# Graph network with routed experts on one core: places of windows packed four to a word, three row buffers, alternating loads, and the leading window added by VectorE from PSUM

## The reference

```python
# first network: two layers of
summed = segment_sum(x[src], dst); cnt = segment_sum(1, dst)
out = (summed / max(cnt, 1)) @ W_l + b_l + x @ W_r        # relu between the two
x = layernorm(x + out)
# second network: h = x @ W_in + b_in, then for 3 layers
agg = segment_sum(h[src], dst) / max(deg, 1)
logits = concat([h, agg]) @ router_W[l] + router_b[l]     # 8 experts, best two, softmax gates
weak   = relu(agg @ weak_W[l, e] + weak_b[l, e])          # 4 experts
strong = relu(agg @ strong_W1 + b1) @ strong_W2 + b2      # 4 experts, 256 -> 512 -> 256
h = h + sigmoid(h @ conf_W + conf_b) * (gates of the two chosen experts times their outputs, summed)
x = layernorm(x + h @ W_out + b_out)
```

## Time and profile before

| | |
|---|---|
| median of 3 runs | 2573.72 us (2569.99 to 2582.82) |
| the profiled execution | 2555.54 us |
| its span, first to last instruction | 2553.7 us |
| TensorE busy | 2043.9 us (80%) |
| VectorE busy | 907.4 us (36%) |
| ScalarE busy | 578.7 us |
| GpSimd busy | 667.3 us |
| mean granted TensorE clock | 0.859 |

### The profile page before, as it was taken

The page is one execution under the profiler, slowest core; times in us unless marked ns, Lnnn a source line. Parts: engine busy times, 40 slices in busy tenths (PEclk is TensorE's granted clock), DMA queues, the critical chain, the costliest instruction groups (busy, mean ns, idle before and its releaser), DMA issues.

```text
span 2553.7 us, 36575 instructions
## 1 busy us (share of the span) xinstructions
PE 2043.9 (80%) x12522; PEld 1588.1 (62%) x12523; DVE 907.4 (36%) x2327; ACT 578.7 (23%) x1160; POOL 667.3 (26%) x611
## 2 busy tenths in 40 slices
PE   2656666509999899888878999888878999888875
PEld 1345555406767677776656777776756777776664
DVE  5566666442234322533332101333332101333323
ACT  0045555540001000222221000232221100222221
POOL 4133443300000013443330111343330112343330
PEclk9855555559999899999998999899998999899996
DMA  6920000197466755343345432243335432243333
GB/s 175 347 77 0 0 0 0 39 390 263 141 184 226 231 190 190 81 74 59 59 79 212 149 121 75 60 80 59 59 73 210 157 120 77 58 75 63 61 51 103
DMA packets 187286, 298.04 MB, mean 117 GB/s; under 512 B 47952, under 2 KB 153094, under 8 KB 187043
## 3 DMA queue, kind: packets, MB, share of 16 engines
q1 hardware_dynamic: 148786, 237.95, 27.8%
q0 software_dynamic: 38384, 58.53, 12.9%
HBM read 179.30 MB, written 117.13 MB: 116 GB/s over the span
## 4 chain that ended last, share of the span: by engine, by line
PE 63%; DMA 15%; DVE 13%; issue 5%; ACT 2%; SPq 1%; DVEq 0%; POOL 0%; ACTq 0%; POOLq 0%
PE psum L1382 20%; PE psum L1498 13%; DMA arena<-xs_d 12%; PE psum L1296 7%; PE psum L1279 6%; DVE arena L729 4%; PE psum L1461 3%; PE psum L1476 2%; DVE arena L1056 2%; DVE arena L1054 2%; PE psum L1250 2%; DMA adj_d<-arena 1%; PE psum L1301 1%; PE psum L1487 1%; PE psum L1275 1%
## 5 line engine op out<-in xcount | busy, mean ns | idle before, releaser
L1382 PE MATMUL psum<-arena 128*128 128x320 bf16 x3750 | 533.1, 306 | 36.4 <-DMA arena<-adj_d 24.4
L1382 PEld LDWEIGHTS psum<-arena 128*128 128x128 bf16 x3750 | 373.9, 100 | 190.7 <-issue 25.2
L646 POOL DMA_INDIRECT h_rows<-arena,idx x192 | 304.0, 1583 | 558.5 <-DVE arena L1056 515.0
L1487 PE MATMUL psum<-arena 128*128 128x256 f32 x1536 | 361.1, 389 | 3.4 <-ACT arena L1208 3.3
L1498 PE MATMUL psum<-arena 128*128 x1536 | 350.3, 381 | 2.6 <-ACT arena L1211 2.2
L1487 PEld LDWEIGHTS psum<-arena 128*128 128x128 f32 x1536 | 281.3, 193 | 67.9 <-ACT arena L1211 19.0
L1498 PEld LDWEIGHTS psum<-arena 128*128 128x128 f32 x1536 | 285.6, 191 | 40.4 <-issue 5.1
L1211 ACT ACTIVATE arena<-psum,b1c 128x256 f32<-128x256 f32 x384 | 181.8, 474 | 490.5 <-PE psum L1487 490.3
L618 POOL DMA_INDIRECT xs_d<-arena,pos x150 | 145.1, 967 | 549.3 <-DVEq L876 507.3
L1296 PE MATMUL psum<-arena 128*128 128x320 bf16 x1500 | 224.9, 302 | 73.7 <-DMA arena<-adj_d 73.7
L729 DVE TENSOR_TENSOR arena<-arena 125x1600 bf16<-125x1600 bf16 x200 | 229.4, 1190 | 135.3 <-PE psum L1279 133.9
(11 more groups left out here) (250 smaller groups left out, 1681.0 us busy)
## 6 DMA issues: line engine op xcount, KB each, us to landing
arena<-adj_d SPq DMA_DIRECT2D x125, 800.0 KB, 4.5
xs_d<-zrow SPq DMA_DIRECT2D x8, 3432.0 KB, 26.7
arena<-xs_d SPq DMA_DIRECT2D x96, 264.0 KB, 3.4
adj_d<-arena SPq DMA_DIRECT2D x25, 800.0 KB, 7.4
arena<-h_rows SPq DMA_DIRECT2D x22, 640.0 KB, 8.7
h_rows<-zrow SPq DMA_DIRECT2D x1, 8192.0 KB, 38.3
arena<-x_d SPq DMA_DIRECT2D x20, 320.0 KB, 3.6
arena<-in_L_gnn_strong_W SPq DMA_DIRECT2D x24, 256.0 KB, 6.7
```

The lines of the kernel that those rows point to most:

```text
L646: pool.indirect_dma_start(h_rows, bass.IndirectOffsetOnAxis(ap=idx[:, j % 2, h:h + 1], axis=0), ybuf[:, j % 2, h], None, compute_op=ALU.ad ...
L1382: mm = pe.matmul(psum[:, q, 0:HN], hs[:, k * SK + s, part, f * P:(f + 1) * P], half(ring[:, k, s], h), start=(k == 0 and s == 0 and part = ...
L1487: mm = pe.matmul(psum[:, 5 + f % 2, 0:M], w1s[:, j % 2, f // 2, kt, f % 2 * P:(f % 2 + 1) * P], xsT[:, j % 2, kt], start=(kt == 0), stop=( ...
```

## The change

Four edits. The diff below is cut to their core; the removed `adds` is GpSimd's, the new one VectorE's.

1. The places of four windows are packed into one word of four bits each, so `w_rel` has 400 words and not 1600. TensorE loads 16 words once for 8 supersteps and takes each place out with shift, mask and multiplication by WP = 103. The windows now lie 103 columns apart in the two banks.
2. The staging copy on ScalarE and the adds on GpSimd go. VectorE adds the leading window straight from PSUM to `adj`. In each iteration the adds of batch q-1 stand behind the one-hots of batch q, and those of the last batch at the iteration's end. TensorE waits for the add of superstep u-4 too.
3. `xsl` has three buffers. The load of slot j waits for the scaling of slot j-3.
4. Units 3 to 7 of the new states and the five pieces of the next layer's first block are issued in turn.

```diff
-        w_rel = carve([T], I32, 1)
+        w_rel = carve([T // 4], I32, 1)
-        xsl = carve([2, 2, XW], F32)
+        xsl = carve([3, 2, XW], F32)
...
-                    if j > 1:
-                        sp.wait_ge(b_yr, 2 * (J - 1))
-                    sp.dma_start(xsl[:, j % 2], ...
+                    if j > 2:
+                        sp.wait_ge(b_yr, 2 * (J - 2))
+                    sp.dma_start(xsl[:, J % 3], ...
...
-                    if u == 3 and p < 4:
-                        expert_pieces(p + 1, 0)
+                    if u >= 3 and p < 4:
+                        expert_pieces(p + 1, 0, (u - 3,))
...
-            def adds(i):
...
-                    pool.wait_ge(s_stage, i * RS + u + 1)
-                    pool.wait_ge(s_wide, i * RS + u + 1)
-                    pool.wait_ge(s_first, i * RS + u + 1)
-                    a = adj[:, bass.ds(off[u], WC)]
-                    pool.tensor_tensor(a, first_w[:, u % 8], a, ALU.add).then_inc(s_first, 1)
...
                     one_hots(i, q)
+                    if q == 0:
+                        _, off = nc.values_load_multi_w_load_instructions(w_off[0:1, bass.ds(i * RS, RS)], ...
+                    else:
+                        adds(i, q - 1, off)
+                adds(i, NOH - 1, off)
+
+            def adds(i, q, off):
+                for g in range(k):
+                    u = q * k + g
+                    v.wait_ge(s_wide, i * RS + u + 2)
+                    v.wait_ge(s_first, i * RS + u + 1)
+                    a = adj[:, bass.ds(off[u], WC)]
+                    v.tensor_tensor(a, psum[:, u % 4 * 2, 0:WC], a, ALU.add).then_inc(s_first, 1)
...
-                    act.copy(first_w[:, u % 8], banks[:, 0, 0:WC]).then_inc(s_stage, 1)
...
-                    if q % 2 == 0:
-                        n = 2 * k * G
-                        _, rel = nc.values_load_multi_w_load_instructions(
-                            w_rel[0:1, bass.ds(i * (NOH // 2 * n) + q // 2 * n, n)], ...
+                    if q == 0:
+                        _, words = nc.values_load_multi_w_load_instructions(
+                            w_rel[0:1, bass.ds(i * (2 * RS), 2 * RS)], ...
...
                             pe.wait_ge(s_wide, i * RS + u - 2)
+                            pe.wait_ge(s_first, i * RS + u - 2)
...
+                            word = words[2 * u + z // 4]
+                            place = word >> 12 if z % 4 == 3 else (word >> 4 * (z % 4)) & 15 if z % 4 else word & 15
+                            place = nc.s_assert_within(place * WP, 0, G * WP, ...
-                            mm = pe.matmul(bank[:, bass.ds(rel[(q % 2 * k + g) * G + z], WC)], ...
+                            mm = pe.matmul(bank[:, bass.ds(place, WC)], ...
```

More of the change, by code:

```diff
@@ L296, in build @@
         b_tab = sem("slot_tables_ready")
-        b_xin = [sem(f"slot_rows_in_{k}") for k in range(2)]
+        b_xin = [sem(f"slot_rows_in_{k}") for k in range(3)]
         b_turn = sem("slot_turned"); b_xT = sem("slot_turned_taken"); b_w1 = sem("slot_weights_ready")
@@ L459, in _, with expert_pieces @@
                     states(p, b)
-            def expert_pieces(p, b):
+            def expert_pieces(p, b, ks=range(NK)):
                 i = blk(p, b)
-                for k in range(NK):
+                for k in ks:
                     if i == 0:
@@ L715, in _ @@
             link(v.tensor_tensor(w4, w4, base.unsqueeze(2).broadcast_to((1, T // G, G)), ALU.subtract))
-            link(v.tensor_scalar(step_no[0:1, 0:T], wf[:, :], 5.0, float(PAD), ALU.is_ge, ALU.mult))
-            v.scalar_tensor_tensor(w_rel[:, :], wf[:, :], float(WC), step_no[0:1, 0:T], ALU.mult, ALU.add).then_inc(s_tab, 1)
+            four = wf[:, :].rearrange("o (s g) -> o s g", g=4)
+            packed = step_no[0:1, 0:T // 4]
+            link(v.scalar_tensor_tensor(packed, four[:, :, 3], 16.0, four[:, :, 2], ALU.mult, ALU.add))
+            link(v.scalar_tensor_tensor(packed, packed, 16.0, four[:, :, 1], ALU.mult, ALU.add))
+            v.scalar_tensor_tensor(w_rel[:, :], packed, 16.0, four[:, :, 0], ALU.mult, ALU.add).then_inc(s_tab, 1)
             v.wait_ge(s_zero, 2)
@@ L1135, in supersteps @@
                 for u in range(RS):
-                    banks = psum[:, u % 4 * 2:u % 4 * 2 + 2]
+                    banks = psum[:, u % 4 * 2:u % 4 * 2 + 2].rearrange("p b n -> p (b n)")
                     act.wait_ge(s_step, i * RS + u + 1)
-                    if not head or u >= 8:
-                        act.wait_ge(s_first, i * RS + u - 6)
-                    act.copy(first_w[:, u % 8], banks[:, 0, 0:WC]).then_inc(s_stage, 1)
                     act.wait_ge(s_wide, i * RS + u + 1)
-                    act.copy(adj[:, bass.ds(off[u] + WC, G * WC)].rearrange("p (b n) -> p b n", b=2), banks[:, :, WC:WC + GA]).then_inc(s_wide, 1)
+                    act.copy(adj[:, bass.ds(off[u] + WC, G * WC)].rearrange("p (w n) -> p w n", w=G),
+                             banks[:, WP:WP + G * WP].rearrange("p (w n) -> p w n", w=G)[:, :, 0:WC]).then_inc(s_wide, 1)
             supersteps(0, head=True)
@@ L1261, in supersteps @@
                 for q in range(NOH):
-                    if q % 2 == 0:
-                        n = 2 * k * G
-                        _, rel = nc.values_load_multi_w_load_instructions(
-                            w_rel[0:1, bass.ds(i * (NOH // 2 * n) + q // 2 * n, n)], engines=(EPE,), min_val=0, max_val=G * WC + PAD,
-                            skip_runtime_bounds_check_because="a window's offset in its superstep")
+                    if q == 0:
+                        _, words = nc.values_load_multi_w_load_instructions(
+                            w_rel[0:1, bass.ds(i * (2 * RS), 2 * RS)], engines=(EPE,), min_val=0, max_val=0x8888,
+                            skip_runtime_bounds_check_because="four windows' places in a superstep, four bits each")
                     pe.wait_ge(s_oh1, i * NOH + q + 1)
@@ L1278, in supersteps @@
                             n = (g * G + z) // 2
[L1279 removed]
+                            word = words[2 * u + z // 4]
+                            place = word >> 12 if z % 4 == 3 else (word >> 4 * (z % 4)) & 15 if z % 4 else word & 15
+                            place = nc.s_assert_within(place * WP, 0, G * WP, skip_runtime_bounds_check_because="a window's place in its superstep")
+                            mm = pe.matmul(bank[:, bass.ds(place, WC)], oh1[:, q, n, :, z % 2], oh2[:, q, n, :, z % 2],
                                            start=False, stop=(z == G - 1), skip_group_check=True)
```

30 lines of the change are left out of this document (12 added, 18 removed).

## The result

The changed kernel takes 2680.4 us (median of 4 runs, 2677.8 to 2695.2), the kernel before, beside it, 2571.9 us (4 runs, 2564.0 to 2582.8). The ratio is **1.043, 95% interval 1.038 to 1.049**: +109 us. The forecast was 2674 us, inside a range of 2600 to 2725; 86 in 100 stood on slower. The profiled execution took 2677.8 us (span 2676.0), 122 us more than that of before. Its build takes 207 us more from first one-hot to last add (107.3 to 692.5 against 121.8 to 499.7), its slots take 78 us less, and each start of a layer lacks the second wait.

The account below looks back on a forecast made before the run. TensorE's sequencer was taken to bound the build. Build +195, row buffer -82 and queue -12 gave +101 us: the profiled 2555.5 became 2656.5, and with 18.2 to the median 2675, stated as 2674 us, range 2600 to 2725.

Parts of the forecast that it names:

- TensorE's sequencer bounds the build: Build of the adjacency: TensorE's sequencer, not the array or another engine, sets the pace in all 25 iterations, 14.73 us each.
- 0.09 us per ALU operation: Build, TensorE's sequencer: each ALU operation costs 0.09 us, and the change adds 80 to an iteration, 7.2 us.
- 8 semaphore waits, 0.9 us: Build, TensorE: the eight added semaphore waits of an iteration cost 0.11 us each, 0.9 us together.
- Longer fused operations, 0.6 us: Build, TensorE: 64 fused operations an iteration get one or two more steps, 0.01 us each, 0.6 us together.
- Iteration without the end gap, 17.9 us: Build: 8.96 us of supersteps plus 7.2, 0.9, 0.6 and 0.2 us make 17.9 us an iteration before its end gap.
- End gap 4.5 us: End of a build iteration: TensorE waits 4.5 us for a chain of wide copy, VectorE's add and next one-hots.
- Third row buffer, -82: Slots: the 88 waits for row loads, 106.3 us, go, the relu is late next, so -82 us.
- Alternating queue, -12: Start of a layer: TensorE's second wait, 6.64 us for VectorE, goes in both transitions, -12 us.
- Sum +101: Whole kernel: 195 us lost in the build, 82 saved in the slots, 12 at layer starts, +101 us.
- A: Rival, build: register operations nearly free, iteration some 16.5 us, in all -49 us, 2525 us; 9 in 100.
- B: Rival, build: no stall for the adds at the iteration's end, gap 2.05 us, +41 us, 2615 us; 10 in 100.
- C: Rival, slots: they keep their waits, in the scatter's landing or slower loads, 2756 us; 6 in 100.

Follow-up runs that it names:

- e8: The kernel before with one more ALU operation of TensorE's sequencer per matmul of the build (a mask that changes nothing): 2690.1 us, ratio 1.058.
- e10: The kernel of e3 with one more, already met semaphore wait on TensorE per superstep of the build: ratio 0.970 to the kernel before.
- e4: The changed kernel with the leading 100 columns staged by ScalarE and added by GpSimd again: 2578.5 us, ratio 1.013 to the kernel before.
- e9: The kernel of e3 with two places packed to a word, ten bits each: ratio 0.982 to the kernel before.
- e7: The changed kernel with the last batch's adds moved behind the next iteration's first one-hots: 2602.2 us, ratio 1.023 to the kernel before.
- e1: The kernel before with three row buffers and nothing else: 2462.8 us, ratio 0.969.
- e2: The kernel before with the alternating queue and nothing else: 2522.9 us, ratio 0.9915.
- e6: The changed kernel with a word for each place again, VectorE's adds kept: 2486.6 us, ratio 0.978 to the kernel before.
- e3: The kernel before with the third row buffer and the alternating queue, its own build kept: 2442.9 us, ratio 0.961.

## Why the prediction was right, step by step

- **TensorE's sequencer bounds the build**: held. One operation more per matmul (e8) lengthens every iteration by its full price.
- **0.09 us per ALU operation**, so 7.2 us an iteration: 0.094 (e8), 7.5 us. The listed length of 0.032 misleads, the distance to the next operation counts.
- **8 semaphore waits, 0.9 us**: 0.73 (e10), or 0.9 by the 0.11 of after against e4.
- **Longer fused operations, 0.6 us**: the mis-sized term. Of 64, the 16 that carry a shift cost some 0.047 us more each (matmul to matmul 0.171 us against 0.124, with no ALU operation between), the other 48 some 0.009: 1.2 us. Rows with 0.068 us at most had hidden that; e9 missed on the same term.
- **Iteration without the end gap, 17.9 us**: 23.45 - 4.2 = 19.2. Of the 1.3 us missing the fused operations explain 0.6 and the ALU operations 0.3. Another 0.2 lies in the base. The 4.48 us were read from one half of an iteration and doubled; over all iterations of before the first half takes 4.49 and the second 4.59. And in after the step to the new batch where the mid gap was takes 0.42 us, 0.32 without the added wait, for the 0.2 that was put in. The last 0.1 to 0.2 isn't assigned.
- **End gap 4.5 us**: 4.2 in after. Its two sides are measured apart: 2.03 us are TensorE's own (e4), and moving the adds gives 2.1 back (e7). The add at 0.26 us was exact. Sum of the build: +207 or 208 us for +195. Here luck helped: the iteration was 0.95 us longer than forecast, which would be 24 us in 25. But the head iteration, which the sum counted like the others, took only 2.2 us more than in before (17.8 against 15.6 us from its first matmul to the loop), and from the first one-hot to the first matmul it took 4 us less. The trace of before has the head's two loads of places at 6.0 and 6.9 us, that of after its one at 1.4.
- **Third row buffer, -82**: -78 (e1, interval -70 to -87, and the slots of after). The relu's 0.75 us took the wait's place, as said; the miss of 4 is within the interval.
- **Alternating queue, -12**: -14 to -30, 22 in the middle (e2). The wait went as said; left out was the granted clock, which falls in such a wait and slows what follows.
- **Sum +101**: +109. The build's loss was put 13 too low, the buffer's gain 4 too high, the queue's gain 10 too low; the last offsets most of the first, which is luck.
- **The rivals.** A fell with e8 and e4, B with e7, C with e1. The 16.5 us that A's working gave for cheap register operations stand beside 16.57 in e6, but by luck. A's working had VectorE's chain pace the later batches, and in e6 it shows only at the iteration's end, 1.1 us, with 0.73 for the waits.

One thing the prediction didn't say: the two parts of the build aren't independent. VectorE's adds cost 42 us with plain places (e6 against e3), but 77 with packed ones (1.0432 against 1.0131). In the plain build the chain over VectorE at the iteration's end lies beside the load of 32 places, 2.13 us; the packed load is 1.1 us shorter, and the chain sticks out. What was saved on the load was handed to the wait.

## What to carry to other kernels

Where an engine is idle on paper and paced by its sequencer, count register operations, fused steps and waits, and price them by the distance between starts of neighbouring operations, not by their listed length. Packing a table to shorten a register load pays only if unpacking takes less than the load saved: here 0.066 us a word against 0.094 for a mask and 0.045 for a shift, so even two places a word lose. Before a step is moved into another engine's loop, look at what stands ahead of its next hand-off, and put it behind.

## What was not expected of the hardware

At the program's start, TensorE's matmuls of 400 columns run at about half their later rate for a time that differs from execution to execution. The windows of before and of after, 64 to 95 us, with the same stream of matmuls since 47 us:

```profile
64.00:95.00 31.00, 31.00 (x86) 1.00 1.09 341
```

```profile
64.00:95.00 31.00, 25.70 (x132) 0.99 1.09 341
```

In before 86 matmuls fill 31 us, 0.36 us each; in after 132 fill 25.7 us, 0.195 us each. The 1.00 of the first row is no clock that was read. The trace's first clock entry, at 1.00, begins at 94.9 us in before, at 63.6 in after and at 78.1 in e10, each time just where the rate doubles, and the windows view counts time without an entry as 1.00. So a rise of the granted clock from the lower level to the upper one fits the slow stretch and its end; the slow stretch itself has no entry that shows the level. The first entry stands at 62 to 64 us in eight of the twelve profiles, at 78 in e10, and at 94 to 95 in before, e6 and e9. Why it comes so much later in some, no row tells.

So the build's first matmul starts at 110.8 us in after and at 129.6 in before. It starts at 111.1 in e1 and at 118.2 in e10, whose work ahead of the build is that of before. A difference between two profiled executions can hold up to 20 us of this, which is no part of the change; the granted clock's column doesn't show it, only the spacing of the matmuls does.
